# Gated cross-attention block: each batch's probabilities and context sums put directly behind its own scores

## The reference

```python
    def _L0_xattn_ref(query, key):
        a = jnp.einsum('bqd,bkd->bqk', query, key)
        e = jax.nn.softmax(a, axis=-1)
        c = jnp.einsum('bqk,bkd->bqd', e, key)
        return c
    ...
    x = x + jnp.tanh(g_xattn[0]) * _L0_xattn_ref(_layernorm(x, axis=-1), ctx_4096)
    x = x + jnp.tanh(g_ffn[0]) * _L0_ffn_ref(_layernorm(x, axis=-1), L0_ffn_qweight, L0_ffn_weight_scale, L0_ffn_weight_zero_point, L0_ffn_bias)
```

## Time and profile before

| | |
|---|---|
| Median of 3 runs | 693.84 us (692.46 to 694.7) |
| Profiled execution | 691.12 us, span 689.1 us |
| Mean granted clock of TensorE | 0.974 |
| PE busy | 637.0 us (92%) |
| DVE, ACT, POOL busy | 247.0, 198.6, 55.9 us |

### The profile page before, as it was taken

One profiled execution on the slowest core, in us unless ns is written; L12 is line 12 of the kernel. 1 busy time (PEld: TensorE's weight loads), 2 busy tenths in 40 slices (PEclk: granted clock), 3 DMA queues, 4 the chain that ended last, 5 costly groups with the idle time before them and its releaser, 6 DMA issues.

```text
span 689.1 us, 7204 instructions
## 1 busy us (share of the span) xinstructions
PE 637.0 (92%) x2936; PEld 342.9 (50%) x2936; DVE 247.0 (36%) x405; ACT 198.6 (29%) x394; POOL 55.9 (8%) x141
## 2 busy tenths in 40 slices
PE   1998999999999999999999999989999299999997
PEld 1666635644653664565466366434444044444443
DVE  2013006114310601522241050271896545564443
ACT  1445503522540541353155044222113212121000
POOL 2001001201200400120030010011100000000000
PEclk9999999999999999999999999999999699999999
DMA  8991058428517534851852681268528949386320
GB/s 254 265 302 57 1 173 267 48 87 283 83 36 259 180 48 148 291 49 32 290 125 42 236 172 32 92 200 184 186 74 219 233 103 252 113 229 127 81 65 35
DMA packets 45998, 102.58 MB, mean 149 GB/s; under 512 B 28958, under 2 KB 28958, under 8 KB 37406
## 3 DMA queue, kind: packets, MB, share of 16 engines
q1 hardware_dynamic: 17806, 76.98, 35.8%
q0 software_dynamic: 3200, 18.85, 13.0%
q10 hardware_dynamic: 24960, 6.29, 5.3%
HBM read 82.71 MB, written 13.11 MB: 139 GB/s over the span
## 4 chain that ended last, share of the span: by engine, by line
PE 87%; DMA 6%; ACT 4%; DVE 2%; issue 1%; SPq 1%; DVEq 0%; ACTq 0%
PE pv L663 25%; PE S L646 21%; PE pv L709 16%; PE T L616 15%; PE S L709 8%; DMA raw<-in_ctx 4%; DMA raw<-xa 1%; ACT qT L350 1%; DVE xT L503 1%; ACT xT L379 1%; ACT raw L350 1%; PE S L723 1%; PE pv L723 1%; SPq L199 0%; ACT ring L350 0%
## 5 line engine op out<-in xcount | busy, mean ns | idle before, releaser
L646 PE MATMUL S<-ring,qT 128*100 128x361 f32 x512 | 195.9, 468 | 0.0
L663 PE MATMUL pv<-raw,pT 128*100 128x512 f32 (+1 forms) x384 | 174.0, 613 | 1.4 <-ACT pT L373 0.8
L350 ACT ACTIVATE ring<-T 128x361 f32<-128x361 f32 x256 | 120.3, 472 | 113.2 <-PE T L616 113.0
L616 PEld LDWEIGHTS T<-ident,raw 128*128 128x128 f32 (+1 forms) x768 | 98.9, 142 | 81.0 <-issue 45.8
L616 PE MATMUL T<-ident,raw 128*128 128x128 f32 (+1 forms) x768 | 122.5, 271 | 6.3 <-DMA raw<-in_ctx 2.9
L663 PEld LDWEIGHTS pv<-raw,pT 128*100 128x100 f32 (+1 forms) x384 | 65.8, 174 | 101.6 <-issue 100.0
L709 PE MATMUL pv<-raw,xT 128*128 128x512 f16 x512 | 111.7, 379 | 0.0
L709 PEld LDWEIGHTS pv<-raw,xT 128*128 128x128 f16 x512 | 49.8, 98 | 61.7 <-issue 2.5
L646 PEld LDWEIGHTS S<-ring,qT 128*100 128x100 f32 x512 | 68.4, 168 | 4.4
L709 PE MATMUL S<-raw,xT 128*128 128x512 f16 x256 | 58.5, 389 | 12.8 <-DMA raw<-xa 12.8
L475 DVE SCALAR_TENSOR_TENSOR xres<-pv,soft,xres 100x512 f32<-100x512 f32 x32 | 24.0, 751 | 108.8 <-PE pv L663 107.0
(11 more groups left out here) (64 smaller groups left out, 312.8 us busy)
## 6 DMA issues: line engine op xcount, KB each, us to landing
raw<-in_ctx SPq DMA_DIRECT2D x32, 1024.0 KB, 4.8
raw<-in_ctx SPq DMA_DIRECT2D x16, 840.0 KB, 5.8
raw<-in_L_ffn_qweight SPq DMA_DIRECT2D x16, 768.0 KB, 6.2
xres<-in_x POOLq DMA_DIRECT2D x8, 800.0 KB, 10.6
x_scratch<-xres POOLq DMA_DIRECT2D x8, 800.0 KB, 7.8
raw<-x_scratch SPq DMA_DIRECT2D x24, 256.0 KB, 4.4
out_y<-raw SPq DMA_DIRECT2D x24, 256.0 KB, 2.5
xa<-in_x POOLq DMA_DIRECT2D x7, 800.0 KB, 6.6
```

The source lines that it names most:

```text
L350: act.activation(dst, src(T[k]), ACT.Copy, **how).then_inc(s_free[k], 1)
L616: last = pe.transpose(dst(T[k]), src, ident[0:n, 0:n])
L646: last = pe.matmul(S[0:R, g, 0:GW], qT[:, c, :], ring[:, (f - 2) % RING, :], start=(c == 0), stop=(c == CH - 1))
L663: last = pe.matmul(pv[n][0:R, :], pT[0:ROWS[t], t, :], raw[0:ROWS[t], b % 2, t, n * 512:(n + 1) * 512], start=(t == 0), stop=(t == NT - 1))
```

## The change

PE's order becomes scores(i), normed(i - 1), queries(i + 1), probs(i), attend(i), for all batches. ACT's and DVE's loops and the table follow: ACT's exponential of batch i stands between the copies of its scores and the copies of the rows; DVE normalizes the rows of `x` one batch ahead instead of two; POOL loads `x` for batch i + 1 in turn i. The last batch has two weight tiles turned between its rows and its probabilities, and the other two within its context sums, ahead of context tiles 2 and 3 instead of 3 and 4; the rows of batch 6 are no longer turned there.

```diff
@@ the numbering of the groups @@
-        order = [("q", 0, 4), ("S", 0, 2 * CH)]
+        order = [("q", 0, 4)]
         for i in range(B):
+            order.append(("S", i, 2 * CH))
+            if i >= 1:
+                order.append(("x", i - 1, 4))
             if i < LAST:
-                order += [("q", i + 1, 4), ("S", i + 1, 2 * CH)]
-            if i == LAST:
+                order.append(("q", i + 1, 4))
+            else:
                 order += [("W", 0, 2), ("W", 1, 2)]
             order.append(("P", i, 2))
-            if 0 < i < LAST:
-                order.append(("x", i - 1, 4))
-        order += [("W", 2, 2), ("W", 3, 2), ("x", LAST - 1, 4)]
+        order += [("W", 2, 2), ("W", 3, 2)]
@@ gpsimd @@
-            next_x(1)
-            rstd(0, 1)
             for i in range(B):
-                if i + 2 < B:
-                    next_x(i + 2)
+                if i + 1 < B:
+                    next_x(i + 1)
                 if i >= 1:
                     x1_out(i - 1)
                     rstd(1, i - 1)
-                if i + 2 < B:
-                    rstd(0, i + 2)
+                if i + 1 < B:
+                    rstd(0, i + 1)
@@ scalar @@
-            context(0)
-            act.wait_ge(s_gate, 32)
-            act.activation(tg[:, 0:2], gates[:, :], ACT.Tanh).then_inc(s_tanh, 1)
-            exps(0)
             for i in range(B):
+                context(i)
+                if i == 0:
+                    act.wait_ge(s_gate, 32)
+                    act.activation(tg[:, 0:2], gates[:, :], ACT.Tanh).then_inc(s_tanh, 1)
+                exps(i)
+                if i >= 1:
+                    rows_hi(i - 1)
                 if i < LAST:
                     queries(i + 1)
-                    context(i + 1)
-                if i == LAST:
+                else:
                     weights(0)
                     weights(1)
                 probs(i)
-                if 0 < i < LAST:
-                    rows_hi(i - 1)
-                if i < LAST:
-                    exps(i + 1)
             weights(2)
             weights(3)
-            rows_hi(LAST - 1)
@@ vector @@
-            ln1_stats(1)
-            ln1_norm(1)
-            row_max(0)
-            coef(0)
             for i in range(B):
                 if i >= 1:
                     residual(i - 1)
                     ln2_stats(i - 1)
                     ln2_center(i - 1)
-                if i + 2 < B:
-                    ln1_stats(i + 2)
-                if i == LAST:
-                    unpack(2)
+                if i < LAST:
+                    ln1_stats(i + 1)
                 if i >= 1:
                     ln2_scale(i - 1)
-                if i + 2 < B:
-                    ln1_norm(i + 2)
                 if i < LAST:
-                    row_max(i + 1)
-                    if i >= 1:
-                        rows_lo(i - 1)
-                    coef(i + 1)
-                if i == LAST - 1:
+                    ln1_norm(i + 1)
+                else:
                     unpack(0)
                     unpack(1)
+                row_max(i)
+                if i >= 1:
+                    rows_lo(i - 1)
+                coef(i)
...
+            unpack(2)
             unpack(3)
-            rows_lo(LAST - 1)
@@ tensor @@
             queries(0)
-            scores(0)
             for i in range(B):
+                scores(i)
+                if i >= 1:
+                    normed(i - 1)
                 if i < LAST:
                     queries(i + 1)
-                    scores(i + 1)
-                if i == LAST:
+                else:
                     weights(0)
                     weights(1)
                 probs(i)
-                if 0 < i < LAST:
-                    normed(i - 1)
                 if i < LAST:
                     attend(i)
-            attend(LAST, {3: lambda: weights(2), 4: lambda: weights(3), 5: lambda: normed(LAST - 1)})
+            attend(LAST, {2: lambda: weights(2), 3: lambda: weights(3)})
```

More of the change, by code:

```diff
@@ L561, in _ @@
             ln1_norm(0)
-            ln1_stats(1)
-            ln1_norm(1)
-            row_max(0)
-            coef(0)
-            dve.tensor_scalar(tg[:, 2:3], tg[:, 1:2], 1.0 / X_SCALE, None, ALU.mult).then_inc(s_tg, 1)
-            dve.wait_ge(s_tg, 1)
             for i in range(B):
@@ L572, in _ @@
                     ln2_center(i - 1)
-                if i + 2 < B:
-                    ln1_stats(i + 2)
-                if i == LAST:
-                    unpack(2)
+                if i < LAST:
+                    ln1_stats(i + 1)
                 if i >= 1:
                     ln2_scale(i - 1)
-                if i + 2 < B:
-                    ln1_norm(i + 2)
                 if i < LAST:
-                    row_max(i + 1)
-                    if i >= 1:
-                        rows_lo(i - 1)
-                    coef(i + 1)
-                if i == LAST - 1:
+                    ln1_norm(i + 1)
+                else:
                     unpack(0)
                     unpack(1)
+                row_max(i)
+                if i >= 1:
+                    rows_lo(i - 1)
+                coef(i)
+                if i == 0:
+                    dve.tensor_scalar(tg[:, 2:3], tg[:, 1:2], 1.0 / X_SCALE, None, ALU.mult).then_inc(s_tg, 1)
+                    dve.wait_ge(s_tg, 1)
+            unpack(2)
             unpack(3)
-            rows_lo(LAST - 1)
             residual(LAST)
@@ L744, in _ @@
                 probs(i)
-                if 0 < i < LAST:
-                    normed(i - 1)
                 if i < LAST:
                     attend(i)
-            attend(LAST, {3: lambda: weights(2), 4: lambda: weights(3), 5: lambda: normed(LAST - 1)})
+            attend(LAST, {2: lambda: weights(2), 4: lambda: weights(3)})
             for nb in range(NB):
```

## The result

| | before | changed |
|---|---|---|
| median | 693.19 us (692.46 to 694.7, 4 runs) | 726.75 us (724.2 to 733.26, 4 runs) |
| ratio | | 1.0495, 95% interval 1.0422 to 1.0569 |
| profiled execution | 691.12 us, span 689.1 | 733.26 us, span 731.3 |
| mean granted clock | 0.974 | 0.932 |

Slower by 33.6 us, where 719.7 us (+26) had been forecast, with a range of 709 to 731.

What follows compares the result with a forecast made beforehand. PE, busy 637.0 of 689.1 us, was taken to set the time, through its work and waits. 691.12 + 17.3 (seams) + 8.6 (clock) = 717.0 us, stated 719.7 as 2.7 above the profiled execution; range 709 to 731.

Steps and rivals of the forecast that it cites:

- The seams' chain: Transposes and copies from S (first instruction behind a score block) to the sums: 8.90 us against 6.38; +17.3 us in all.
- Batch 7: Last batch's turns: rows' 5.09 us, then weights and probabilities 5.57, 10.66 us where 8.43 were paid: +2.2 us.
- The clock: PE's clock falls once in each of seven long seams, 2.35 us each, 16.5 less today's 7.9: +8.6 us.
- The rival with two falls per seam: Two clock falls in a row behind each long seam, +19.7 us instead of +8.6: 728.1, stated 730.8; chance 0.15.
- the 8.9 to 10 that I gave as a sign: Middle batch, first row turn to first context sum matmul: 8.9 to 10 us expected in the profile, against 4.03 before.
- Batch 0, nothing: First batch's seam: queries, probabilities, sums with the same 1.46 us behind the queries as before; no added time.
- Nothing from context loads, cover on VectorE: Context loads win nothing (2.9 us of waits, at the start); VectorE readies rows and queries with at least 14 us cover.
- Weight tiles: Weight tiles 2 and 3, turned within batch 7's sums, come one context tile earlier, at no cost.
- The output stage moves as a block: Everything behind the last context sums hangs on their end in both kernels, so that stretch stays alike.
- The rival "faster": Maximum and exponential hide beside row and query turns; a seam costs 4.86 us instead of 6.38: 674.1, stated 677; chance 0.05.
- A fall in every one of the seven long seams: Sign expected in the profile: granted clock of 0.5 in or behind every long seam between scores and sums.

Runs made afterwards that it cites:

- the kernel with fillers: Changed kernel with thrown-away products in the seam's pauses (two behind the second row turn, one behind the fourth, batches 1 to 7): 710.81 us, ratio 1.0234.
- the fastest kernel: Kernel before with row and query turns put between the context sums' products, ScalarE's exponential moved ahead of the row copies: 675.79 us, ratio 0.9731.

## Why the prediction was right, and where it was off

- *The seams' chain, +17.3 us*: right. Each step came where it was worked out while the clock was at 1.00: third row turn S + 3.22 (3.16), sums S + 9.07 (8.90) in the kernel with fillers. Doubling and moving the exponential showed its place in the chain. Batch 7: 34.7 us in the kernel with fillers and 32.3 before, each with 1.4 us in a slow start of its sums: +2.4 (+2.2 forecast).
- *The clock, +8.6 us*: the right mechanism, mis-sized. The 7.9 us of five falls, which the sum subtracts, are read from durations in the earlier trace rows. The windows of the kernel before show the falls: its six middle seams all have the pauses of 0.40 and 0.72 us, and at the end of four of them the clock goes from 1.00 to 0.50 for some 3.4 us (the earlier trace rows is of batch 2's), while it stays at 1.00 in the other two, of which the earlier trace rows is one; the fifth is batch 7's (0.50 in the windows from 462 to 465). I priced one fall per seam, 1.6 us behind it and 0.75 in slowed turns, 2.35 in all. In the profile of the changed kernel the six seams are 61.2 us instead of 6 x 9.07 = 54.4, the six blocks 137.9 instead of 123.7, batch 0's 2.7 us over 20.66, batch 7 3.8 us over: 27.6 us at eight places, 3.5 each, where the kernel before lost 9.2 (7.9 and 1.3 in batch 1's scores). So +18 instead of +8.6 in this execution; by the medians it is 33.6 - 18.5 for the chain = +15, the output stage's wait included. The clock comes down within the seam, near S + 3.4 in batch 1 and S + 5.6 in batch 2, and comes back only in the sums, 3.2 and 5.9 us behind their start. The rival with two falls per seam (3.95 each, stated 730.8) described that better than the forecast did; the measured 726.75 lies between them. Its mechanism is not what happened, though: in the windows of batches 1 and 2 there is one fall each, a long one. The step that was mis-sized is the cost of one fall. I gave it 0.75 us in the seam and 1.6 behind it; in the mean of the six middle batches it is 1.1 in the seam (61.2 - 54.4) and 2.4 in the sums (137.9 - 123.7), since once down the clock stays down through the rest of the seam and into the sums, some 10 us where, in the block of the earlier trace rows, a low lasted about 3.4 us (0.72 in the window 202 to 203, 0.57 in 205 to 206). For the same reason four of the six seams, at 10.04 to 10.48 us, are over the 8.9 to 10 that I gave as a sign.
- *Batch 0, nothing*: off by 1.7 us. The fall behind its seam now hits the sums (23.40 instead of 20.66 us; the clock is at 0.50 in the windows from 57 to 63) instead of batch 1's scores (31.19, now 29.90; there it was at 0.50 from 56 to 59).
- *Nothing from context loads, cover on VectorE*: right. VectorE has the queries of batch 3 ready 13.3 us behind the start of batch 2's scores (16.9 less the 3.57 us that fell away), and PE waits for neither rows nor queries. Timeline of DVE:

```profile
155.82 1.35 DVE L451 TENSOR_SCALAR xa<-xa,mr 100x2048 f32<-100x2048 f32 x1 [1.74 <-POOL mr L307]
```

- *Weight tiles*: I had both coming one context tile earlier; only tile 2 does. It costs nothing that shows, since batch 7 comes out at +2.4 us without the clock.
- *The output stage moves as a block*: not quite; its one wait for transposed weights varied by up to 4.6 us with the changed order. Open, as said above.
- *The rival "faster"* was wrong for the reason given: exponential over at S + 2.06, not at S + 0.85. Its idea holds if the copies come first, and then only in part (715.31 us).
- *A fall in every one of the seven long seams*: right. In the changed kernel the clock is at 0.50 in windows in or behind each of the seven. With fillers, where the same turns have no pause over 0.64 us instead of one of 2.12, it stays at 1.00 through the six middle ones of the profiled execution; behind batch 7's it is at 0.50 in the windows from 479 to 481.

## What to carry to other kernels

When PE is 92% busy, as here, a new order is judged by what PE waits for at its borders, and there by what stands in front of each copy in the copying engine's queue (12.9 us for the place of one exponential). Software pipelining that keeps a reduction and its exponential a whole block ahead of their use was worth more here than a tidier order: 30.6 us with the turns inside the sums in both. Where groups of transposes must be copied out, put them between long products one group at a time instead of several in a row: that was worth 18 us here, in waits and in clock.

## What the runs showed of the hardware that was not expected

- Work without use made the kernel faster: 21 thrown-away products took 17.4 us off the median of the changed kernel, and 6 took about 6 us off the one before (0.9902).
- With pauses of 0.40 and 0.72 us among short transposes the clock came down to 0.50 in four of six seams of the kernel before; in the changed kernel, with one of 2.1 us, it came down in all seven, but also in all seven with the rows copied first, where no pause is over 0.82 us. With a pause of 0.72 us between probabilities and sums alone, and long blocks on both sides, it stayed at 1.00 in all six middle batches of the fastest kernel.
- In the changed kernel the lower clock slows not only products but also the seam, through the transposes that the copies wait for: the same ten groups of turns took 9.07 us with the clock at 1.00 and 10.48 with the clock at 0.66 in the mean.
